# Six and three PSUM banks for the edge sums, rings of 14 and 10 groups of gathered rows

## The reference

```
x = x + gnn0(layernorm(x), edge_attr_64, src, dst)  # sum over edges of [n[src], edge] @ W, relu, norm, 3-layer MLP, norm
x = x + moe0(layernorm(x))                          # 16 experts, the 2 best of each token, relu, norm
x = x + gnn1(layernorm(x), src, dst)                # n@W_self + mean over edges of top32(n@W_neigh)[src]
x = x + moe1(layernorm(x))                          # 8 experts, the 2 best of each token, gelu
```

## Time and profile before

| | |
|---|---|
| median of 3 runs | 2111.38 us (2108.23 to 2117.15) |
| the profiled execution | 2116.55 us |
| its span, first to last instruction | 2114.8 us |
| TensorE busy | 1290.4 us (61%) |
| GpSimd busy | 1096.2 us (52%) |
| VectorE busy | 725.1 us (34%) |
| ScalarE busy | 389.2 us (18%) |
| mean granted TensorE clock | 0.781 of 2.4 GHz |

### The profile page before, as it was taken

One profiled execution on the slowest core, in us unless ns is written; L12 is line 12 of the kernel. 1 busy time (PEld: TensorE's weight loads), 2 busy tenths in 40 slices (PEclk: granted clock), 3 DMA queues, 4 the chain that ended last, 5 costly groups with the idle time before them and its releaser, 6 DMA issues. The chain is left out here.

```text
span 2114.8 us, 29212 instructions
## 1 busy us (share of the span) xinstructions
PE 1290.4 (61%) x7947; PEld 1141.0 (54%) x7948; DVE 725.1 (34%) x2200; ACT 389.2 (18%) x1296; POOL 1096.2 (52%) x1166
## 2 busy tenths in 40 slices
PE   0268787877878439999655633455465455368820
PEld 0267677777768428999622222455454454266710
DVE  4122444444444360111189921222222222431123
ACT  0000111111111103444344400000000000024433
POOL 2666666556664003222387556666666666033355
PEclk9778888888888669999855656676777776689965
DMA  6334434334343009999622123333333333059955
GB/s 172 102 103 112 110 105 115 107 106 110 103 111 96 9 29 358 353 351 345 221 73 80 58 76 91 89 98 96 97 100 96 96 100 95 17 169 299 316 164 149
DMA packets 230156, 289.67 MB, mean 137 GB/s; under 512 B 76686, under 2 KB 181152, under 8 KB 229782
## 3 DMA queue, kind: packets, MB, share of 16 engines
q1 hardware_dynamic: 178994, 154.64, 22.7%
q0 software_dynamic: 48192, 131.35, 22.1%
q10 hardware_dynamic: 2852, 2.24, 0.5%
HBM read 256.41 MB, written 32.04 MB: 136 GB/s over the span
## 5 line engine op out<-in xcount | busy, mean ns | idle before, releaser
L743 POOL DMA_INDIRECT O0G<-n_rows,src_tab x392 | 387.9, 990 | 264.8 <-issue 144.6
L743 POOL DMA_INDIRECT O1G<-sparse_rows,src_tab x392 | 378.2, 965 | 199.9 <-issue 120.3
L758 PE MATMUL O1ps_sums<-O1OH,O1G 128*128 128x128 f32 x1568 | 264.9, 340 | 139.7 <-issue 63.1
L758 PEld LDWEIGHTS O1ps_sums<-O1OH,O1G 128*128 128x128 f32 x1568 | 251.9, 252 | 147.4 <-issue 147.4
L758 PE MATMUL O0ps_sums<-O0OH,O0G 128*128 128x128 f32 x1568 | 228.8, 298 | 56.4 <-issue 39.4
L758 PEld LDWEIGHTS O0ps_sums<-O0OH,O0G 128*128 128x128 f32 x1568 | 212.1, 212 | 67.5 <-issue 67.3
L779 DVE TENSOR_TENSOR sumT<-sumT,O1ps_sums 128x256 f32 x98 | 41.2, 420 | 443.4 <-remote 322.9
L779 DVE TENSOR_TENSOR sumT<-sumT,O0ps_sums 128x384 f32 x98 | 54.2, 554 | 342.0 <-remote 191.4
L1335 POOL DMA_INDIRECT e0xs<-token_rows,e0idx x64 | 60.7, 948 | 205.1 <-ACT e0idx L1395 204.0
L758 PE MATMUL O0ps_sums<-O0OH,O0EA 128*128 128x128 f32 x784 | 117.2, 293 | 27.2 <-issue 27.1
L1358 PE MATMUL e0ps_h<-e0xT,e0W 128*128 128x128 f32 x1024 | 126.6, 277 | 1.1 <-DMA e0W<-in_L_ffn_w 1.1
(11 more groups left out here) (297 smaller groups left out, 1984.8 us busy)
## 6 DMA issues: line engine op xcount, KB each, us to landing
e0W<-in_L_ffn_w SPq DMA_DIRECT2D x128, 512.0 KB
e1W<-in_L_ffn_w SPq DMA_DIRECT2D x112, 256.0 KB
O0EA<-in_edge_attr SPq DMA_DIRECT2D x97, 128.0 KB
expert_out<-e0ys SPq DMA_DIRECT2D x64, 128.0 KB
expert_out<-e1ys SPq DMA_DIRECT2D x56, 128.0 KB
O0G<-n_rows,src_tab POOLq DMA_INDIRECT x392
O1G<-sparse_rows,src_tab POOLq DMA_INDIRECT x392
n_rows<-NR SPq DMA_DIRECT2D x5, 640.0 KB
```

The source lines that it names most:

```text
L743: pool.indirect_dma_start(out=self.G[:, s, k, :], out_offset=None, in_=self.rows_dram, in_offset=bass.IndirectOffsetOnAxis(ap=src_tab[:, g ...
L758: last = nc.tensor.matmul(self.ps[o % 2][:, half * P:(half + 1) * P], rows, self.OH[:, h, k, :], start=(k == 0), stop=(k == GC - 1))
```

## The change

`Sums` gets its sizes from the caller: rows (the ring G), hots (the ring of one-hot tiles), edges (the ring of edge features) and banks (PSUM banks for the products).

| | before | O0 after | O1 after |
|---|---|---|---|
| slots of gathered rows | 8 | 10 | 14 |
| one-hot tiles | 4 | 5 | 8 |
| slots of edge features | 4 | 6 | none in use |
| banks for products | 2 | 3 | 6 |
| one-hot tiles ahead of the add | 2 | 3 | 6 |

The banks come from the node layers. In O0, layers 0 and 1 share one bank, so layer 0 of a tile waits for relu1 of the tile before instead of relu0, and layer 1 has no such wait. In O1, the transposes of N4 and the logits share one, so the transposes wait for `logits_in` of the tile before instead of `nT_ready`, and the logits have no such wait. Both stages then use all eight banks.

```diff
-            def __init__(self, tag, c, rows_dram, with_edges):
+            def __init__(self, tag, c, rows_dram, with_edges, rows, hots, edges, banks):
...
-                self.G = sb(tag + "G", [P, GR, GC, D], F32, c)
-                self.EA = sb(tag + "EA", [P, ER, GC, P], F32, c) if with_edges else None
-                self.OH = sb(tag + "OH", [P, HR, GC, P], F32, c)
-                self.ps = [pb(f"{tag}ps_sums{b}", [P, 512], c) for b in range(2)]
+                assert hots > banks
+                self.rows, self.hots, self.edges, self.banks = rows, hots, edges, banks
+                self.G = sb(tag + "G", [P, rows, GC, D], F32, c)
+                self.EA = sb(tag + "EA", [P, edges, GC, P], F32, c) if with_edges else None
+                self.OH = sb(tag + "OH", [P, hots, GC, P], F32, c)
+                self.ps = [pb(f"{tag}ps_sums{b}", [P, 512], c) for b in range(banks)]
...
             def gather(self, pool, o):
-                g, s = NG - 1 - o, o % GR
-                if o >= GR:
-                    pool.wait_ge(self.summed, o + 1 - GR)
+                g, s = NG - 1 - o, o % self.rows
+                if o >= self.rows:
+                    pool.wait_ge(self.summed, o + 1 - self.rows)
...
             def products(self, pe, o):
...
-                if o >= 2:
-                    pe.wait_ge(self.added, o - 1)
+                if o >= self.banks:
+                    pe.wait_ge(self.added, o + 1 - self.banks)
...
             def add(self, dve, o):
-                self.hot(dve, o + 2)
+                self.hot(dve, o + self.banks)
...
-                        sums.hot(dve, 0)
-                        sums.hot(dve, 1)
+                        for o in range(sums.banks):
+                            sums.hot(dve, o)
...
-                self.ps_agg, self.ps_tn, self.ps_0, self.ps_1, self.ps_2, self.ps_bg = (
-                    pb(f"{tag}ps_{n}", [P, 512], c) for n in ("agg", "turned", "0", "1", "2", "back"))
+                self.ps_agg, self.ps_tn, ps_01, self.ps_2, self.ps_bg = (
+                    pb(f"{tag}ps_{n}", [P, 512], c) for n in ("agg", "turned", "01", "2", "back"))
+                self.ps_0, self.ps_1 = ps_01[:, 0:D], ps_01[:, D:2 * D]
...
                     wait_tile(pe, S["hT_ready"], t)
-                    wait_tile(pe, S["relu0"], t, 1)
+                    wait_tile(pe, S["relu1"], t, 1)
                     layer(0, self.ps_0, s, S["first"])
...
                     wait_tile(pe, S["added0"], t)
-                    wait_tile(pe, S["relu1"], t, 1)
                     layer(1, self.ps_1, s, S["second"])
...
-                self.ps_s, self.ps_n, self.ps_g = (pb(tag + n, [P, 512], c) for n in ("ps_s", "ps_n", "ps_g"))
+                self.ps_s, ps_ng = (pb(tag + n, [P, 512], c) for n in ("ps_s", "ps_n"))
+                self.ps_n, self.ps_g = ps_ng[:, 0:D], ps_ng[:, D:2 * D]
...
                     wait_tile(pe, S["n_ready"], t)
-                    wait_tile(pe, S["nT_ready"], t, 1)
+                    wait_tile(pe, S["logits_in"], t, 1)
                     turn2(self.ps_n, self.N4[:, s, :], S["n_turned"])
...
                     wait_tile(pe, S["nT_ready"], t)
-                    wait_tile(pe, S["logits_in"], t, 1)
...
-        sums_and_nodes("O0", n_dram, True, NodeMlp)
+        sums_and_nodes("O0", n_dram, True, NodeMlp, dict(rows=10, hots=5, edges=6, banks=3))
...
-        sums_and_nodes("O1", hs_dram, False, NeighbourMeans)
+        sums_and_nodes("O1", hs_dram, False, NeighbourMeans, dict(rows=14, hots=8, edges=0, banks=6))
```

More of the change, by code:

```diff
@@ L19 @@
 GU = 7
-GR = 8
-HR = 4
-ER = 4
 BU = 4
@@ L713, in build @@
         class Sums:
-            def __init__(self, tag, c, rows_dram, with_edges):
+            def __init__(self, tag, c, rows_dram, with_edges, rows, hots, edges, banks):
                 self.rows_dram, self.with_edges, self.halves = rows_dram, with_edges, 3 if with_edges else 2
-                self.G = sb(tag + "G", [P, GR, GC, D], F32, c)
-                self.EA = sb(tag + "EA", [P, ER, GC, P], F32, c) if with_edges else None
-                self.OH = sb(tag + "OH", [P, HR, GC, P], F32, c)
-                self.ps = [pb(f"{tag}ps_sums{b}", [P, 512], c) for b in range(2)]
-                self.gathered = [held_sem(f"{tag}gathered{s}") for s in range(GR)]
-                self.edges_in = [sem(f"{tag}edges_in{s}") for s in range(ER)]
+                assert hots > banks
[4 more added lines that the diff above has]
+                self.ps = [pb(f"{tag}ps_sums{b}", [P, 512], c) for b in range(banks)]
+                self.gathered = [held_sem(f"{tag}gathered{s}") for s in range(rows)]
+                self.edges_in = [sem(f"{tag}edges_in{s}") for s in range(edges)]
                 self.hot_ready, self.summed, self.added, self.ones_set = (
@@ L728, in load_edges @@
             def load_edges(self, sp, o):
-                g, s = NG - 1 - o, o % ER
-                if o >= ER:
-                    sp.wait_ge(self.summed, o + 1 - ER)
+                g, s = NG - 1 - o, o % self.edges
+                if o >= self.edges:
+                    sp.wait_ge(self.summed, o + 1 - self.edges)
                 if g == NG - 1:
@@ L747, in products @@
             def products(self, pe, o):
-                r, h, e = o % GR, o % HR, o % ER
+                r, h, ps = o % self.rows, o % self.hots, self.ps[o % self.banks]
                 pe.wait_ge(self.hot_ready, o + 1)
                 if self.with_edges:
-                    pe.wait_ge(self.edges_in[e], (o // ER + 1) * 16)
-                pe.wait_ge(self.gathered[r], (o // GR + 1) * 16 * GC)
-                if o >= 2:
-                    pe.wait_ge(self.added, o - 1)
+                    e = o % self.edges
+                    pe.wait_ge(self.edges_in[e], (o // self.edges + 1) * 16)
+                pe.wait_ge(self.gathered[r], (o // self.rows + 1) * 16 * GC)
+                if o >= self.banks:
+                    pe.wait_ge(self.added, o + 1 - self.banks)
                 for half in range(self.halves):
@@ L757, in products @@
                         rows = self.EA[:, e, k, :] if half == 2 else self.G[:, r, k, half * P:(half + 1) * P]
-                        last = nc.tensor.matmul(self.ps[o % 2][:, half * P:(half + 1) * P], rows, self.OH[:, h, k, :],
+                        last = nc.tensor.matmul(ps[:, half * P:(half + 1) * P], rows, self.OH[:, h, k, :],
                                                 start=(k == 0), stop=(k == GC - 1))
@@ L764, in hot @@
                     return
-                if o >= HR:
-                    dve.wait_ge(self.summed, o + 1 - HR)
+                if o >= self.hots:
+                    dve.wait_ge(self.summed, o + 1 - self.hots)
                 nc.vector.tensor_tensor(
-                    self.OH[:, o % HR, :, :], iota_w[:].unsqueeze(1).to_broadcast([P, GC, P]),
+                    self.OH[:, o % self.hots, :, :], iota_w[:].unsqueeze(1).to_broadcast([P, GC, P]),
                     rel_tab[:, NG - 1 - o, :].unsqueeze(2).to_broadcast([P, GC, P]),
@@ L778, in add, with sums_and_nodes @@
                 window = sumT[:, 0:self.halves, ds(base, P)]
-                nc.vector.tensor_tensor(window, window, self.ps[o % 2][:, 0:self.halves * P].rearrange("p (h w) -> p h w", h=self.halves),
+                nc.vector.tensor_tensor(window, window, self.ps[o % self.banks][:, 0:self.halves * P].rearrange("p (h w) -> p h w", h=self.halves),
                                         ALU.add).then_inc(self.added, 1)
-        def sums_and_nodes(tag, rows_dram, with_edges, Stage):
+        def sums_and_nodes(tag, rows_dram, with_edges, Stage, rings):
             with ExitStack() as c:
-                sums, stage = Sums(tag, c, rows_dram, with_edges), Stage(tag, c)
+                sums, stage = Sums(tag, c, rows_dram, with_edges, **rings), Stage(tag, c)
                 block = c.enter_context(nc.Block())
```

## The result

The changed kernel takes 2139.20 us (median of 4 runs, 2133.51 to 2142.03) against 2111.18 us before (4 runs): ratio 1.0128, with an interval of 1.0101 to 1.0155. It is 28 us slower; forecast were 2107 us and a gain of 4. The profiled run is the lowest of the four, 2133.51 us with a span of 2131.8 us, so the two traces differ by only 17.0 us of the 28.

What follows compares the result with a forecast made beforehand. Gathers were taken to hold back TensorE's work or its report, so a stage costs gathers, needed pauses and the remainder. Terms 4.5 + 9.8 - 18.4 = -4.1 us gave 2107 us, range 2045 to 2140 us.

Steps and rivals of the forecast that it cites:

- The frame: O0 and O1: each costs 490 us of gathers, plus the pauses TensorE needs, plus what is left after the last gather.
- TensorE's work, or the report of it: O0 and O1: one of these is held back while gathers run and catches up in GpSimd's pauses; no size given.
- Rings: Gathers running further ahead move work from pauses to the end: +4.5 us in O0, +9.8 us in O1.
- Banks in O1: Six banks for two, one-hot tiles as far ahead: freed waits shorten GpSimd's pauses, -18.4 us.
- Runs with pauses joined: O1 after 1393 us: seven pairs of gather runs join, each saving 0.7 us, in all 5 us.
- Costed at nothing: Waits from shared banks in both stages and additional one-hot tiles ahead of the first add: no time charged.
- Layer 0 behind relu1: O0 node layers: wait for relu1 of the tile before has 7.9 us of cover, costs nothing; uncovered, 0.63 us a tile.
- The transposes behind the copied logits: O1, N4: wait has 1.7 us of cover, costs nothing; a copy 2 us late in 25 tiles would cost 50 us.
- C: O1: the ring alone counts, banks bring under 4 us; +14.3 us, 2126 us, up to 2146 us; chance 0.22.
- A: O1: banks are the limit, all 56.0 us of add waits go, ring's +14.3 us remain; -42 us, 2070 us; chance 0.25.
- B: Both stages: lateness is not the gathers' doing, GpSimd runs through, pauses go; -178 us, 1934 us; chance 0.06.
- D: Both stages: nothing is felt, the end gets what the start had; within 4 us of 2111; chance 0.10.

Runs made afterwards that it cites:

- a chip without pauses: Changed kernel with rings of 8, its banks kept, against the kernel before, on a chip where GpSimd never paused: ratios 1.0035 and 1.0031.
- a limit at the end: Kernel before with rings of 10 and 14, last 16 groups at most 4 ahead: with pauses 2112.67 us against 2094.72, ratio 1.0089.
- the second chip: Changed kernel and kernel before, both unaltered, on another chip with pauses: 2109.82 us against 2092.13, +17.7 us.

## Why the prediction was wrong

**The frame held.** Gathers, pauses and the rest behind the last gather are the whole of a stage, and TensorE catches up only when GpSimd stands. "TensorE's work, or the report of it" left open which: it is the report first, and some 30 us into a stage, with some 32 passes unreported, the work too, 7 to 9 passes in 20 us. The measured 2139.2 us lie just inside the range, 2045 to 2140, but on the other side of the kernel before than was forecast.

The Trainium skill (SBUF — State Buffer, Who interferes with whom) has TensorE wait on nobody. The trace of after disagrees, with 23 passes in 60 us late in a run of gathers and 63 in the 10 us from GpSimd's restart; a chip without pauses agrees, with 64 in 20 us. That section speaks of ports into SBUF, and whether a port is what holds TensorE no run here shows.

**Rings: right, as a term.** Forecast +4.5 and +9.8, 14.3 us in all; measured +15.3 with the rings alone (12 to 20), though against another chip's trace O0 had more of it than forecast (+9.7). In the traces of before and after, of the parts in O1: left for the end 7 groups more and 18.1 us (forecast 6 groups, 14.9 us), pauses 5.0 us less (forecast 6 x 0.84 = 5.0). In O0: 2 groups and 5.5 us more (forecast 7.1), pauses 0.4 us less (forecast 2.6). The first pause came after 18 groups, where some 17 were named. So the prices a group fit; that a limit at the end gained nothing shows that the groups are lost in the first run, which the sum did not say.

**Banks in O1: the step that failed.** "with more products per pause I take 10 us off", 5 for joined pairs and 3.4 at the first run's end, -18.4 us, came out as +3.8 us (-0.4 to +7.6), of which about 3 lie in the barrier. The wait for adds went, all 56.0 us, as forecast. But the step took it that products freed of that wait would be done, and reported, in GpSimd's pauses, and so shorten them. They were recorded earlier and reported no earlier: with rings of 8, an add of O1 comes up to 36.0 us behind its group with six banks and up to 36.8 with two, and behind some 32 unreported passes TensorE goes on at one pass per 1.4 to 2.8 us. So 127.0 us of "issue" ahead of L760 stand where 63.1 and the 56.0 us for adds stood.

Runs with pauses joined were forecast as a gain of 0.7 us each; with the banks alone the pauses of O1 are 25, where the two traces of before have 37 and 32, and the pace of 5.7 us a group is the same. TensorE still stands 106.5 + 14.8 us at L1713, where 145 us was named. The prediction had the sign of this in its rows: adds that idle for a signal and come with GpSimd's stops. More banks do not bring that signal forward, and the price should have been nothing.

**Costed at nothing.** Layer 0 behind relu1: TensorE stands ahead of L963 for 5.0 us of "issue" and 1.4 us for hT in O0, and none for relu1. The transposes behind the copied logits: none in the steady part. In the last tiles of O1, where no group lies between, VectorE's wait for the next logits grows from 1.85 to 2.34 us a tile. The barrier's 3.5 us were in no sum.

**Rivals.** C, that in O1 the ring alone counts, is what happened, and the 2139 us lie in its 2126 to 2146; its condition, banks that bring under 4 us, was met. A and B fell: the pauses of O1 are 74.7 us. D fell. Shown are the rings' +15.3 and the banks' +3.8, 19.1 us together, which fits the 17.7 us of the second chip. The first result's 28 us (21 to 33) are 9 more; the intervals overlap, and its trace, of the lowest run, doesn't show them.

The Trainium skill (Perfetto Trace Analysis, Matmul Optimizations) wants all eight PSUM banks in use; here six banks for two in one stage together with three for two in the other gained nothing: 1.0017 with pauses and 1.0033 (mean of two) without.

## What to carry to other kernels

A look-ahead ring is worth its first few slots, enough to cover the landing of the data: 4 were enough here, 2 were not. Where the producer slows its consumer, each slot more lets it run on at the start of the stage, and comes back as a group that must be done when the producer stops. Try a shorter ring before a longer one. And a wait that disappears from the profile is a gain only if the engine then works at its full pace and its signals come sooner: look for what stands next in its queue, and for passes that come one by one.

## What was not expected of the hardware

- Beside back-to-back indirect DMAs of GpSimd, on the chips with pauses, TensorE's signals came up to 68 us after the recorded end of the work, and after some 30 us it fell from groups of 16 passes in 3.75 us to single passes 1.4 to 2.8 us apart, and kept to that for some 6 us into GpSimd's stop. No trace has more than 32 passes between a group's last one and its add. The clock isn't it: at 0.50 (the level of 1.2 GHz) a pass took 0.37 us instead of 0.27. The rows had landed, and the traffic was 105 GB/s, as on the chips where nothing of it shows. Nor is it code that was being fetched: the packets of the instruction queues nearest to that stretch start at 1266.1 and 1346.5 us. What holds the signals is open; gathers spaced apart, or rows fetched by another kind of DMA, were not tried.
- The same program took 1903 us on three chips and 2092 to 2112 us on the others. Nearly all of it lies in the two stages with gathers: with the banks alone, from the first gather to the last add, 511.1 and 503.7 us instead of 630.6 and 581.2, which is 197 of the 204 us between the two spans (1907.6 and 2111.8 us). What sets the chips apart stays open.
- The barrier behind O1 takes about 3 us more in each kernel with both shared banks, 9.8 to 10.3 against 12.9 to 13.6 us. Why is open.
